# Attention and feed-forward block: wider DRAM rows, fp32 q for the first unit, two loads issued by ScalarE

## The reference, cut to what matters

```
x: 4 x 1024 x 512 fp32
n  = layernorm(x);  q, k, v = split(n @ w_qkv.T + b_qkv)            # 16 heads of 32
per chunk of 128 tokens, state S per head:
    inter  = (q * decay_q) @ S
    scores = (q @ k.T) * mask;  intra = scores @ v
    S      = lam**128 * S + (k * decay_k).T @ v
x  = x + layernorm((inter + intra) @ w_out.T + b_out)
n  = layernorm(x);  g = silu(n @ e4m3(gate_w) * gate_s);  u = n @ e4m3(up_w) * up_s
x  = x + layernorm((g * u) @ e4m3(down_w) * down_s)
```

## Time and profile before

| | us |
|---|---|
| median of 3 runs (lowest, highest) | 987.7 (987.54, 988.84) |
| the profiled execution | 988.57 |
| its span, first to last instruction | 986.8 |
| first product of a projection (L767) | 22.64 |
| first product of the attention (L795) | 243.72 |
| TensorE idle from 0 to 20 / from 20 to 200 / in the whole span | 4.15 / 0 / 28.1 |
| VectorE busy from 20 to 60 (of 40) | 38.35 |
| mean granted clock, share of full speed | 0.995 |
| window 18 to 20: granted clock | 0.50 |
| window 8 to 10: GB/s of the DMA engines | 418 |

### The profile page before, as it was taken

How to read it: one execution, slowest core, us unless ns; L and a number is a source line. 1 busy time by engine, 2 the same in 40 slices (tenths; PEclk the granted TensorE clock), 3 DMA queues, 4 the chain that set the end, 5 groups by cost and what they waited for, 6 DMA issues and landing times.

```text
span 986.8 us, 22045 instructions
## 1 busy us (share of the span) xinstructions
PE 958.7 (97%) x8498; PEld 708.9 (72%) x8498; DVE 690.4 (70%) x1359; ACT 509.1 (52%) x985; POOL 687.6 (70%) x837
## 2 busy tenths in 40 slices
PE   8999999999998999999999999999999999999996
PEld 6777777786766777767677676767767676776764
DVE  7999998875887675767667576766757676665422
ACT  3656665565654544636354463635446363544522
POOL 2699998986775675849567584947758594775733
PEclk9999999999999999999999999999999999999999
DMA  9899899999983983847658284766828476512200
GB/s 322 210 290 265 255 276 293 277 254 297 229 207 88 202 180 56 196 93 163 131 127 176 61 194 94 163 128 129 191 48 193 92 165 125 127 52 43 41 26 22
DMA packets 297642, 159.88 MB, mean 162 GB/s; under 512 B 141632, under 2 KB 272832, under 8 KB 297408
## 3 DMA queue, kind: packets, MB, share of 16 engines
q1 hardware_dynamic: 296672, 157.86, 67.4%
q10 hardware_dynamic: 864, 0.61, 0.2%
HBM read 82.93 MB, written 41.94 MB: 127 GB/s over the span
## 4 chain that ended last, share of the span: by engine, by line
PE 57%; DVE 17%; POOL 11%; issue 10%; ACT 4%; DMA 1%; POOLq 0%; DVEq 0%; SPq 0%; ACTq 0%
PE bank L892 17%; PE bank L874 12%; PE bank L767 8%; PE att L767 7%; PE bank L782 7%; POOL att_pool L1059 4%; DVE stats L1326 3%; DVE p L1367 3%; DVE state_hl L1397 3%; DVE w_pool L1460 2%; POOL rstd L998 2%; ACT w_pool L596 2%; POOL w_pool L1077 2%; PE att L851 1%; DVE state L1386 1%
## 5 line engine op out<-in xcount | busy, mean ns | idle before, releaser
L874 PE MATMUL bank<-f_pool,gate_q 128*128 128x256 f16 x1536 | 185.0, 274 | 4.3 <-ACT w_pool L596 3.8
L874 PE MATMUL bank<-f_pool,up_q 128*128 128x256 f16 x1536 | 183.7, 273 | 1.5
L892 PE MATMUL bank<-down_q,w_pool 128*128 128x512 f16 x768 | 168.3, 379 | 0.0
L874 PEld LDWEIGHTS bank<-f_pool,gate_q 128*128 128x128 f16 x1536 | 147.4, 98 | 27.0 <-ACT w_pool L596 6.5
L874 PEld LDWEIGHTS bank<-f_pool,up_q 128*128 128x128 f16 x1536 | 149.4, 98 | 22.4 <-DVE w_pool L1460 5.1
L1059 POOL TENSOR_TENSOR att_pool<-p,att_pool 128x512 f16<-128x512 f32 x128 | 145.7, 1159 | 28.0 <-ACT att_pool L548 27.9
L1460 DVE SCALAR_TENSOR_TENSOR w_pool<-bank,us_t,w_pool 128x256 f32<-128x256 f32 x192 | 84.1, 479 | 112.5 <-ACT w_pool L596 54.7
L995 POOL TENSOR_TENSOR rstd<-mv,eps_t 128x1 f32<-128x1 f32 (+1 forms) x112 | 30.1, 269 | 181.3 <-DVE mv L1329 181.3
L892 PEld LDWEIGHTS bank<-down_q,w_pool 128*128 128x128 f16 x768 | 74.0, 98 | 86.9
L1077 POOL TENSOR_TENSOR w_pool<-w_pool 128x512 f16<-128x512 f32 x96 | 111.3, 1165 | 28.0 <-ACT w_pool L602 27.9
L548 ACT CAST att_pool<-p 128x512 f16<-128x512 f32 x128 | 75.7, 615 | 62.4 <-DVE p L1367 62.3
(11 more groups left out here) (145 smaller groups left out, 1826.4 us busy)
## 6 DMA issues: line engine op xcount, KB each, us to landing
xr<-in_x SPq DMA_DIRECT2D x32, 512.0 KB, 4.6
dram_qk<-qk_hl SPq DMA_DIRECT2D x64, 256.0 KB, 3.7
att_pool<-dram_qk SPq DMA_DIRECT2D x64, 256.0 KB, 5.3
f_pool<-dram_qk SPq DMA_DIRECT2D x64, 256.0 KB, 5.6
dram_kd<-kd_hl SPq DMA_DIRECT2D x32, 256.0 KB, 2.9
dram_v<-vv SPq DMA_DIRECT2D x32, 256.0 KB, 3.7
qn_pool<-dram_qk SPq DMA_DIRECT2D x32, 256.0 KB, 6.2
out_x<-w_pool SPq DMA_DIRECT2D x32, 256.0 KB, 2.3
```

What stands on the lines that cost most here:

```text
L874: ins = nc.tensor.matmul(b[:, j * TOK:(j + 1) * TOK], w[:, k, o * P:(o + 1) * P], x1_hl[:, v % 2, part, k], start=(k == 0 and part == 0), ...
L892: ins = nc.tensor.matmul((b_gate, b_up)[t][:, :], h_hl[:, part, k, t * P:(t + 1) * P], down_q[:, k], start=(k == 0 and part == 0), stop=(k ...
```

## The change

- q, k and kd lie in DRAM by partition: a row of a partition is 1024 fp16 numbers, 2 KB. Spills and loads go by such rows. Column g * 128 + p of the transposed kd becomes column 4 * p + g, so that the state products take every fourth column (8 bytes apart) as stationary operand. The score products take another slot of the stack.
- x of unit 0 is loaded and normalised tile by tile. TensorE transposes the normalised tiles itself into PSUM (`turn_first`), ScalarE copies them to `x_first`, and q of unit 0 is four groups of four fp32 products of 256 columns, from the raw weights. The bias and the result are scaled afterwards in `q_hi`. 58 constant products stay (40, 6, 12), in place of 136.
- ScalarE's `w_hi` and VectorE's `w_lo` go in the order k, v, q. ScalarE normalises x of unit 1 after the two steps for k. The maximum of the bias of v is taken from a third part of `bqk`. The loads of bv and of the three feed-forward scales are issued by ScalarE after its work on x of unit 0.
- From unit 3 on ScalarE issues `load_x(k + 3)` at the head of `ahead(k)`, and `load_piece(k + 3)` at its end. Before, SyncE issued them.

```diff
-        dram_qk = nc.dram_tensor("dram_qk", [units, 2, 2, KT, P, TOK], F16, kind="Internal").ap()
-        dram_kd = nc.dram_tensor("dram_kd", [units, 2, KT, P, TOK], F16, kind="Internal").ap()
+        dram_qk = nc.dram_tensor("dram_qk", [units, 2, 2, P, KT * TOK], F16, kind="Internal").ap()
+        dram_kd = nc.dram_tensor("dram_kd", [units, 2, P, KT * TOK], F16, kind="Internal").ap()
...
+        x_first = f_magic[0][:, 0:KT * TOK].rearrange("p (k t) -> p k t", k=KT)
...
             def spill_q(n):
-                    sp.dma_start(dram_qk[n, 0, part].rearrange("k p t -> p k t"), qk_hl[:, part, 0:KT]
+                    sp.dma_start(dram_qk[n, 0, part], qk_hl[:, part, 0:KT].rearrange("p k t -> p (k t)")
...
             def load_stack(s, which, parts):
-                    sp.dma_start(stacks[s % 2][DH * r:DH * (r + 1), which],
-                                 dram_qk[s, which, parts[r]].rearrange("g (j d) t -> d (g j) t", d=DH)
+                    sp.dma_start(stacks[s % 2][DH * r:DH * (r + 1), which].rearrange("d (j g) t -> d j (g t)", g=KT),
+                                 dram_qk[s, which, parts[r]].rearrange("(j d) f -> d j f", d=DH)
...
             def load_kt(s):
-                                       dram_kd[s].rearrange("s g p t -> (s g p) t")).then_inc(kt_in[s % 2], 16)
+                                       dram_kd[s].rearrange("s p (g t) -> (s p g) t", g=KT)).then_inc(kt_in[s % 2], 16)
...
             def ahead(k):
-                if k + 3 < units:
-                    load_x(k + 3)
                 if k:
                     spill_v(k - 1)
-                    if 3 <= k + 2 < 12:
-                        load_piece(k + 2)
...
-            load_x(0)
+            for t, landed in enumerate((x_first_in, x_in[0])):
+                sp.dma_start(x_src(0)[:, t], x_u[0, :, t]).then_inc(landed, 16)
...
+            def load_x(n):
+                at_least(act, x_lo_d, 2 * (n - 1))
+                act.dma_start(x_src(n), x_u[n]).then_inc(x_in[n % 2], 16)
+            def load_piece(n):
+                at_least(act, f_q_d, n - 2)
+                act.dma_start(stage_for(n), piece_in(n)).then_inc(f_in[n % 3], 16)
...
-            act.dma_start(bv[:, :], b_v).then_inc(bias_in, 16)
+            act.wait_ge(eps_d, 3)
+            nc.scalar.activation(small[:, 63:64], eps_t[:, 0, 0:1], ACT.Silu)
+            x_normalise_tile(0, 0)
+            x_hi_tile(0, 0)
+            x_normalise_tile(0, 1)
+            x_first_tile(0)
+            x_hi_tile(0, 1)
+            x_first_tile(1)
+            act.dma_start(bv[:, :], b_v).then_inc(bv_in, 16)
             act.dma_start(gs_t[:, :], gate_s).then_inc(scl_in, 16)
...
-            for part in range(3):
+            for part in (1, 2, 0):
                 for half in range(2):
                     w_hi(third(wqkv_hi, part, half), third(w_stage, part, half))
-            x_normalise(1)
-            x_hi(1)
+                if part == 1:
+                    x_normalise(1)
+                    x_hi(1)
...
             def ahead(k):
+                if k + 3 < units:
+                    load_x(k + 3)
...
                 kd_hi(k)
+                if 3 <= k + 3 < 12:
+                    load_piece(k + 3)
...
+            def turn_first(t):
+                pe.wait_ge(nrm_d[LN_X], t + 1)
+                for k in range(KT):
+                    ins = nc.tensor.transpose(b_s[t][:, k * P:(k + 1) * P], x_src(0)[:, t, k * P:(k + 1) * P], eye)
+                ins.then_inc(x_first_mm, 1)
+            def project_first(o):
+                for k in range(KT):
+                    ins = nc.tensor.matmul(qk_bank(0, o // 2)[:, o % 2 * TOK:(o % 2 + 1) * TOK],
+                                           w_stage[:, k, o * P:(o + 1) * P], x_first[:, k], start=(k == 0),
+                                           stop=(k == KT - 1))
+                if o % 2:
+                    ins.then_inc(qk_mm, 1)
...
             def project_qk(n, i):
-                if i == 0:
+                if i == 0 or n == 0 and i == 2:
                     pe.wait_ge(*x_landed(n))
+                if n == 1 and i == 0:
+                    pe.wait_ge(w_lo_d, 6)
...
             def project_v(n, t):
                 if n == 0:
-                    pe.wait_ge(w_lo_d, 6)
+                    pe.wait_ge(w_lo_d, 4)
...
                 if has_state(s, c):
+                    k_cols = kt[s % 2][:, c].rearrange("t s (f g) -> t s g f", g=KT)
...
-                                                   kt[s % 2][:, c, a, g * P:(g + 1) * P], v_halves[:, heads(g), b],
+                                                   k_cols[:, a, g], v_halves[:, heads(g), b],
...
-            for n in range(100):
-                nc.tensor.matmul(b_up[:, 0:2 * P], warm[:, 0:P], warm, start=True, stop=True)
-            spread_w_max()
-            for n in range(36):
-                nc.tensor.matmul(b_up[:, 0:2 * P], warm[:, 0:P], warm, start=True, stop=True)
+            constant_products(40)
+            pe.wait_ge(eye_in, 16)
+            turn_first(0)
+            constant_products(6)
+            turn_first(1)
+            constant_products(12)
+            pe.wait_ge(x_first_d, 2)
+            for k in range(KT):
+                pe.wait_ge(w_in[k], 16)
+            project_first(0)
+            spread_w_max()
+            project_first(1)
+            project_first(2)
+            project_first(3)
...
             def prepare_qkv():
+                dve.wait_ge(bias_in, 16)
+                link(nc.vector.tensor_reduce(col(7), bqk[:, :], AX.X, ALU.max, apply_absolute_value=True))
+                nc.vector.tensor_scalar(col(4), col(7), 1.0 / 256.0, None, ALU.mult)
...
-                    if k == 1:
-                        dve.wait_ge(bias_in, 16 * N_BIAS)
-                        nc.vector.tensor_reduce(col(7), bqk[:, :], AX.X, ALU.max, apply_absolute_value=True)
-                        link(nc.vector.tensor_reduce(col(8), bv[:, :], AX.X, ALU.max, apply_absolute_value=True))
-                        link(nc.vector.tensor_tensor(col(7), col(7), col(8), ALU.max))
-                        nc.vector.tensor_scalar(col(4), col(7), 1.0 / 256.0, None, ALU.mult)
...
+                dve.wait_ge(bv_in, 16)
                 link(nc.vector.tensor_scalar(bv[:, :], bv[:, :], col(11), None, ALU.mult))
```

More of the change, by code:

```diff
@@ L324, in spill_k @@
                 for part in range(2):
-                    sp.dma_start(dram_qk[n, 1, part].rearrange("k p t -> p k t"), qk_hl[:, part, KT:2 * KT]
+                    sp.dma_start(dram_qk[n, 1, part], qk_hl[:, part, KT:2 * KT].rearrange("p k t -> p (k t)")
                                  ).then_inc(k_spilled, 16)
@@ L330, in spill_kd @@
                 for part in range(2):
-                    sp.dma_start(dram_kd[n, part].rearrange("k p t -> p k t"), kd_hl[:, part]
+                    sp.dma_start(dram_kd[n, part], kd_hl[:, part].rearrange("p k t -> p (k t)")
                                  ).then_inc(kd_spilled, 16)
@@ L357, in load_q @@
                 for part in range(2):
-                    sp.dma_start(qn[:, s % 2, part], dram_qk[s, 0, part].rearrange("k p t -> p k t")
+                    sp.dma_start(qn[:, s % 2, part].rearrange("p k t -> p (k t)"), dram_qk[s, 0, part]
                                  ).then_inc(q_in[s % 2], 16)
@@ L506, in q_hi @@
                     ins = nc.scalar.activation(q32[:, i, j], qk_bank(n, i)[:, j * TOK:(j + 1) * TOK],
-                                               ACT.Identity, bias=bqk[:, o:o + 1])
+                                               ACT.Identity, bias=bqk[:, o:o + 1],
+                                               scale=1.0 if n else small[:, 11:12])
                 ins.then_inc(q_d, 1)
@@ L747, in spread_wout_max, with constant_products @@
                 ins.then_inc(wout_max_all, 1)
+            def constant_products(count):
+                for n in range(count):
+                    nc.tensor.matmul(b_up[:, 0:2 * P], warm[:, 0:P], warm, start=True, stop=True)
+            def turn_first(t):
[10 more added lines that the diff above has]
+                    ins.then_inc(qk_mm, 1)
             def project_qk(n, i):
-                if i == 0:
+                if i == 0 or n == 0 and i == 2:
                     pe.wait_ge(*x_landed(n))
+                if n == 1 and i == 0:
+                    pe.wait_ge(w_lo_d, 6)
                 if n < LEAD:
@@ L763, in project_qk @@
                     for k in range(KT):
-                        if n == 0 and j == 0 and (i == 0 and k % 2 == 0 or i == 2 and k == 0):
-                            pe.wait_ge(w_lo_d, i + k // 2 + 1 if i == 0 else 4)
+                        if n == 0 and i == 2 and j == 0 and k % 2 == 0:
+                            pe.wait_ge(w_lo_d, k // 2 + 1)
                         for q, (a, b) in enumerate(((0, 0), (0, 1), (1, 0))):
@@ L795, in scores @@
                         ins = nc.tensor.matmul(b_s[g % 2][:, j * P:(j + 1) * P],
```

(31 more changed lines are left out.)

42 lines of the change are left out of this document (29 added, 13 removed).

## The result

The changed kernel is **slower**: 991.92 us median of 7 runs (990.46 to 993.69) against 987.71 (987.48 to 988.84), a ratio of 1.0039 (95% interval 1.003 to 1.0049). The forecast was 983.0 with a range of 980.0 to 987.5. The profiled execution took 993.69 us with a span of 991.9. It is the slowest of the seven, so its trace shows the loss a little large.

The account below looks back on a forecast made before the run. TensorE's own stream bounds the kernel once fed, so only its 22.64 us start can be won: 6.5 us earlier, 5.0 after VectorE, 4.7 after x of unit 3, other terms 0; 987.7 becomes 983.0, range 980.0 to 987.5.

Parts of the forecast that it names:

- First q: Start, TensorE: sixteen fp32 products for q of unit 0 take 7.1 us, 1.9 us more work, beginning at 12.3.
- The scale: Start: the weights' scale is ready at 18.2 us (17.4 to 19.3), where it was 19.26.
- T: The time at which the weights' scale is ready at the start: 18.2 us forecast, 19.26 before.
- Halves of the weights, unit 0: Start: v of unit 0 ends on TensorE at 31.8, so unit 1 could start 6.5 us earlier.
- VectorE: End of the start: VectorE starts unit 2 at 29.9, k_lo(0, 3) still ends near 41.1; 5.0 of 6.5 us stay.
- Loads issued by ScalarE ... Cost 0: Each unit: two more issues, 1.2 us of ScalarE's queue in 15.66 us, covered by its idle time; cost 0.
- x of unit 3: Transposition behind unit 1's spills leaves 4.2 us of room; the middle, 4.7 us of gain, was taken.
- 2-KB rows, 0 in the later stages: Slots: faster spills give 0, as no TensorE wait names a DMA; bounds 0 and 1.5 us in all.
- The clock: Start: pauses before 12.3 may lower TensorE's granted clock during q, costing up to 1.8 us there; net cost 0.
- Strided weight loads: State products: 336 loads with a column every 8 bytes cost 0, as column count is unchanged; bound 14.4 us.
- D: Rival: ScalarE's in-order queue eats the gain, load_x holding k_hi back until VectorE is late; 987.5 us, chance 0.11.
- Slower: Rival: strided weight loads of the state products stop hiding; 997.4 us at the full 43 ns a load, chance 0.09.

Follow-up runs that it names:

- e1: The changed kernel with SyncE issuing the loads of x and of the feed-forward pieces where it did before: 984.63 us, ratio 0.9956.
- e5: As e1, with x of unit 1 transposed at the start ahead of weight pieces 1 and 2 and the output weights: 984.32 us, ratio 0.9956.
- e6: The changed kernel with ScalarE issuing its loads later, after k_hi(k, 2), and with the start of e5: 984.50 us, ratio 0.9957.
- e9: The changed kernel, ScalarE's loads where the change put them, with only the start of e5: 990.04 us, ratio 1.002.
- e2: The kernel before with only the loads of x and of the pieces moved to ScalarE as in the change: 994.26 us, ratio 1.0053.
- e3: The kernel before with only the 2-KB rows and what they bring, strided state products included: 988.88 us, ratio 0.9999.
- e8: The kernel before with only the changed start (fp32 q, new order of weight halves), 512-byte rows and SyncE's loads: 995.08 us, ratio 1.0064.
- e10: As e6, with k_lo(k, 3) ahead of the rounding of a weight piece on VectorE in units 0 and 1: 983.65 us, ratio 0.9956.
- e7: The kernel before, SyncE issuing load_x(k + 3) and load_piece(k + 2) right ahead of the transposition of unit k + 2: 1030.18 us, ratio 1.0417.
- e11: The changed kernel with the start of e5, ScalarE issuing only the feed-forward pieces at the changed place, SyncE x: 987.29 us, ratio 0.9991.
- e12: The changed kernel with the start of e5, ScalarE issuing only x at the changed place, SyncE the pieces: 987.11 us, ratio 0.9985.
- e4: The changed kernel with ScalarE issuing its loads later, after k_hi(k, 2): 987.82 us, ratio 0.9994.

## Why the forecast was wrong, point by point

- **First q**: right. 16 products took 7.2 us (7.1 forecast), from 12.47 (12.3). The 1.1 us freed by the later loads was a small slip: 512 KB at 418 GB/s are 1.25 us.
- **The scale**: T is 17.25, as the reciprocal of L1297 ends there and the first `w_hi` begins at 17.29. That is 1 us before my 18.2 and just under my low bound of 17.4, since x of unit 1 was there by 14.6 and not at 15.5.
- **Halves of the weights, unit 0**: right. v ended at 31.55 (31.8).
- **VectorE**: near in e1 and e5, where TensorE gains 5.65 and 4.5 us up to the first score product (5.0 forecast). The limit by `k_lo(0, 3)` shows in e5 and e6 as a wait of 1.14 us; in e1 the wait is for turned x. VectorE started on unit 2 at 28.84 in e1 (29.9 forecast); in the changed kernel at 31.55, as x of unit 2 lands late. So without the moved loads the sum comes out: 0.9956 of 987.71 is 983.4, for 983.0. Luck has a part in it, since e1 started with an unpriced wait of 1.39 us and an earlier VectorE.
- **The failed step is "Loads issued by ScalarE ... Cost 0".** I costed the issues on the queue that they are moved to, and the waits behind them there. I never asked what the transfers land in front of. SyncE's old place for `load_x` and `load_piece` was behind one transposition and 6 to 11 us ahead of the next (e1, unit 3); the new one is 1.6 to 3.4 us ahead of it. It costs 6.3 us with the early transposition (e9 against e5), 8.2 in the changed kernel as it stands, its start included (e1), and 5.2 alone (e2).
- **x of unit 1** had no step at all. I placed its transposition by when x was ready and gave the landing no price. Ready 6.2 us earlier, it met the start's large loads: a pair of 3.29 us before became 11.39. TensorE lost 4.45 us of waiting and 2.2 by the clock to it in the profiled run. Over many runs e9 puts the share of the changed kernel's start at about 2.
- **x of unit 3**: the right place to look, but with the old length of the transposition, 4.15 us, as the worst case. It became 7.17, and TensorE waited 1.45 us.
- **2-KB rows, 0 in the later stages**: right alone (e3), wrong beside the new start (e8). My argument, that no wait of TensorE names a DMA, held for the old timing only.
- **The clock**: q ran at full clock, after a pause of 1.41 us; in e9's trace, after one of 3.71 us, it did not. The half-rate stretch came at unit 1 instead, after the wait, and cost 2.2 us of the profiled run.
- **Strided weight loads**: right at 0, but my reason was wrong: with the number of columns unchanged, a load takes 113 ns and not 98. The longer load stays hidden. Both cited pages of the Trainium skill allowed the step ("TensorE: Matmul & The Clock Gate", "Weight-path perf modes"; "SBUF — State Buffer", "Door 1: The DMA port swizzle"). The trace agrees for the time of the products, 0.83 us for 12, and not for the load itself.
- **The rivals**: none was it. D had ScalarE's queue as the place of the harm, but by waits of ScalarE, and ended at no change. Slower had 0.09, on the strided loads alone.

The change as three parts, by ratio: rows 0.9999, start 1.0064, loads 1.0053, start and rows 0.9956, all three 1.0039. They don't add up. A version with ScalarE's loads at another moment and the transposition first (e6), or with no load moved (e1, e5), is 0.4% faster than the kernel before and 0.8% faster than the changed one.

## What to carry to other kernels

When a DMA is moved to another queue, ask at which moment it is now issued and which short, awaited transfer it lands in front of; the queue itself was free here (e6), the moment cost 6.2 us (e9 against e6). When one engine is made earlier, price every transfer that it awaits again at its new time of issue, among the traffic that is in flight then, and not by its old length. A part that is worth nothing alone can be what another part's gain rests on.

## What the runs showed of the hardware

- A pair of DMA transpositions (SBUF to SBUF) took SyncE mostly 2.6 to 3.3 us at units 2 to 6 with no large load issued just before (the kernel before, e1, e3, e5, e6, e10; up to 4.46 at single units, and 2.97 to 4.04 in e8). With one load of 0.5 or 0.75 MB issued just before it took 3.8 to 5.2 (e7 at unit 2, e11, e12; 6.95 once), and with both 5.15 to 8.2. The mean of units 3 to 6 is 6.05 us where the loads came from the same queue (e7) and 6.7 and 7.0 where they came from the other (e2, e9). The runs don't tell what in the DMA engines holds it.
- From 160 to 185 us, where the busy share of the DMA engines is 1.05 to 1.08, SyncE needs 2.3 us (e8) or 1.4 us (the kernel before) to issue a spill of 256 KB in 512-byte rows, and 0.45 us (e1, e3) in 2-KB rows. From 40 to 120 us it is 0.51 to 0.57 us against 0.44 to 0.46.
- A stationary operand with a column every 8 bytes loads in 113 ns against 98 (e3).
- Kernels in which ScalarE issues loads spread far: 984.2 to 991.8 in e4, 985.0 to 989.9 in e11, 988.5 to 993.4 in e9, against 984.2 to 985.1 in e5. With one trace of each, what differs from run to run isn't shown.
